# A new order table for every engine of a transformer layer, with the rests of the softmax weights shared out anew

## What is computed

```python
q, k = rope(x @ wq + bq), rope(x @ wk + bk)          # 16 heads of 8
scores = einsum('bhqd,bhkd->bhqk', q, k) / sqrt(8) + causal
attn = softmax(scores) @ (x @ wv + bv)
x = layernorm(x + attn @ wo + bo)
logits = x @ wg; idx = argmax(softmax(logits))         # top-1 of 8 experts
mask = one_hot(idx) * (locations < 512)                # place of the token in its expert
gate = sum(probs * mask)
x = layernorm(x + gate * (x @ W[idx].T + b[idx]))      # for the kept tokens
```

## Time and profile before

| | us |
|---|---|
| median of 3 runs (553.79 to 554.85) | 554.53 |
| the profiled execution | 555.73 |
| its span, first to last instruction | 554.0 |
| TensorE busy | 371.6 |
| VectorE busy | 362.1 |
| ScalarE busy | 246.1 |
| POOL busy | 299.2 |

### The profile page before, as it was taken

One profiled execution on the slowest core, in us unless ns is written; L12 is line 12 of the kernel. 1 busy time (PEld: TensorE's weight loads), 2 busy tenths in 40 slices (PEclk: granted clock), 3 DMA queues, 4 the chain that ended last, 5 costly groups with the idle time before them and its releaser, 6 DMA issues.

```text
span 554.0 us, 13276 instructions
## 1 busy us (share of the span) xinstructions
PE 371.6 (67%) x4150; PEld 317.0 (57%) x4150; DVE 362.1 (65%) x929; ACT 246.1 (44%) x568; POOL 299.2 (54%) x524
## 2 busy tenths in 40 slices
PE   4456478676767768666775775776686576868572
PEld 3344367565746657565655665664575565656551
DVE  5578466774857767584866758486675848584635
ACT  3434545444535345353534545344454445454510
POOL 6344646446383755638284654728465473636433
PEclk9586887988888788888898888889878888878687
DMA  4779548393938365483926547392837439501000
GB/s 115 127 148 128 115 115 98 92 114 98 116 74 136 61 123 63 100 105 92 128 54 127 60 121 78 97 123 64 140 51 133 55 98 115 99 2 43 11 9 21
DMA packets 155055, 50.53 MB, mean 91 GB/s; under 512 B 113567, under 2 KB 151331, under 8 KB 155022
## 3 DMA queue, kind: packets, MB, share of 16 engines
q1 hardware_dynamic: 149118, 45.80, 49.9%
q10 hardware_dynamic: 5184, 2.36, 2.2%
q0 software_dynamic: 720, 1.97, 1.2%
HBM read 30.70 MB, written 14.68 MB: 82 GB/s over the span
## 4 chain that ended last, share of the span: by engine, by line
POOL 28%; issue 21%; DVE 18%; PE 15%; SPq 7%; ACT 5%; DMA 3%; POOLq 1%; DVEq 1%; ACTq 0%
DVE low L868 4%; POOL rs L476 4%; DVE row_max L877 4%; POOL low L515 4%; SPq L419 3%; POOL rot L596 3%; POOL rot_rest L602 2%; POOL y_out L489 2%; POOL all_parts L504 2%; POOL two_parts L502 2%; PE ps_ab L1083 2%; PE ps_m L1019 2%; DVE z L843 2%; PE ps_n L1130 1%; PE ps_m L1020 1%
## 5 line engine op out<-in xcount | busy, mean ns | idle before, releaser
L674 ACT ACTIVATE high<-ps_ab 128x448 f16<-128x448 f32 (+1 forms) x192 | 101.2, 527 | 151.8 <-PE ps_ab L1083 146.9
L877 DVE TENSOR_REDUCE row_max<-ps_ab 128x2 f32<-128x512 f32 (+3 forms) x176 | 108.7, 635 | 73.3 <-PE ps_ab L1093 73.3
L515 POOL TENSOR_TENSOR low<-probs,high 128x448 f16<-128x448 f32 (+1 forms) x80 | 78.7, 984 | 39.2 <-ACT probs L681 39.1
L1063 PE MATMUL ps_ab<-mask_b_bf,ident_bf 128*128 128x128 bf16 (+1 forms) x192 | 51.9, 270 | 58.5 <-DVE low L868 58.3
L1109 PE MATMUL ps_pv<-v_mov,high 128*128 128x64 bf16 x768 | 76.4, 204 | 9.0 <-DVE low L868 8.6
L868 DVE TENSOR_TENSOR low<-ps_ab,high 128x448 f16<-128x448 f32 (+1 forms) x112 | 67.0, 598 | 20.4 <-ACT ps_ab L681 20.4
L1083 PE MATMUL ps_ab<-q_plain,k_diag 128*128 128x128 bf16 (+1 forms) x768 | 78.5, 234 | 0.0
L1109 PE MATMUL ps_pv<-v_mov,low 128*128 128x64 bf16 x768 | 75.3, 203 | 0.0
L1093 PE MATMUL ps_ab<-k_plain,q_diag 128*128 128x192 bf16 (+3 forms) x512 | 74.6, 265 | 0.0
L1109 PEld LDWEIGHTS ps_pv<-v_mov,high 128*128 128x128 f16 x768 | 63.0, 106 | 16.7 <-DVE low L868 10.4
L502 POOL TENSOR_TENSOR two_parts<-pv_rows 128x128 f32<-128x128 f32 x32 | 14.7, 459 | 105.6 <-DVE inv_den L853 105.3
(11 more groups left out here) (178 smaller groups left out, 939.4 us busy)
## 6 DMA issues: line engine op xcount, KB each, us to landing
plain_parts<-rot SPq DMA_DIRECT2D x180, 64.0 KB, 2.0
k_plain<-plain_parts SPq DMA_DIRECT2D x16, 384.0 KB, 3.8
q_diag<-plain_parts SPq DMA_DIRECT2D x32, 192.0 KB, 5.1
q_plain<-plain_parts SPq DMA_DIRECT2D x16, 384.0 KB, 6.0
k_diag<-plain_parts SPq DMA_DIRECT2D x32, 192.0 KB, 6.5
v_mov<-v_parts SPq DMA_DIRECT2D x64, 48.0 KB, 2.2
x_in<-in_L_attn_x_dram SPq DMA_DIRECT2D x16, 128.0 KB, 2.2
x_res<-in_L_attn_x_dram SPq DMA_DIRECT2D x16, 128.0 KB, 2.3
```

The source lines that it names most:

```text
L515: pool.tensor_tensor(fine(low, k), kept_probs(k), fine(high, k), ALU.subtract).then_inc(s_["low_pool"], 1)
L674: act.activation(fine(high, k), b_scores(k), ACT.Exp, scale=SCALE)
L877: last = dve.tensor_reduce(row_max[:, NBLK - 1 - j, groups[0]:groups[-1] + 1], scores[:, :, col:col + width(j)], AX.X, ALU.max)
L1063: return pe.matmul(v, ident_bf[:, :], rows, start=True, stop=False, skip_group_check=True)
```

## The change

Every program step is now divided into 64 slots, and a table for each engine (`PE_AT`, `ACT_AT`, `DVE_AT`, `POOL_AT`) gives each piece a position; `position // 64` is by how many program steps the piece lags behind the start of its sequence, and `position % 64` its slot. `due` finds what stands in a slot. `LAST_AT` holds other positions for the last two sequences. Only the order of each engine's list follows from the numbers. SyncE's list is as it was. Blocks 3 and 9 get their rests on another path: TensorE subtracts `high` from the bank by a product with minus the identity, and ScalarE copies the result out. Block 10's rest goes from POOL to VectorE and block 11's from VectorE to POOL. The routing mask moves from VectorE to ScalarE (`route`), the bias row of the projection becomes three bfloat16 rows, and `x1` gets two buffers. Core of the diff:

```diff
-LOW_POOL = (1, 3, 5, 8, 10)
-B_SLOT, LOW_SLOT, SLOTS = 1, 2, NB + 4
+LOWS = "DPDADPDDPADP"
+SLOTS = 64
+PE_AT = dict(
+    b=(201, 204, 207, 213, 220, 223, 228, 231, 236, 240, 241, 248),
...
+        def bank_free(eng, c, k):
+            if LOWS[k] == "P":
+                after(eng, "exp_done", c, NB, k + 1)
             else:
-                after(eng, "low_dve", c, N_DVE, dve_lows(k) + 1)
+                low_ready(eng, c, k)
...
+                    for k, c, _, _ in due(ACT_AT, "low", *now):
+                        if LOWS[k] == "A":
+                            after(act, "subtracted", c, lows_of("A"), lows_of("A", k + 1))
+                            act.activation(fine(low, k), b_scores(k), ACT.Copy).then_inc(s_["low_act"], 1)
...
+                    for _, d, _, _ in due(ACT_AT, "route", *now):
+                        after(act, "loc_ready", d, 1, 1)
+                        after(act, "kept_done", d, 1, 1)
+                        act.activation(route[0:E, :], ps_route, ACT.Copy, bias=-BIG, scale=BIG).then_inc(s_["route_done"], 1)
...
+                    for k, c, _, _ in due(PE_AT, "sub", *now):
+                        if LOWS[k] == "A":
+                            after(pe, "exp_done", c, NB, k + 1)
+                            pe.matmul(b_scores(k), minus_ident[:, :], fine(high, k), start=False, stop=True,
+                                      skip_group_check=True).then_inc(s_["subtracted"], 1)
...
-                            mm = pe.matmul(ps_n[:, 128 * t:128 * t + 128], row_0[:, :], out_row[:, :],
+                            mm = pe.matmul(ps_n[:, 128 * t:128 * t + 128], rows_1[:, :], out_rows[:, :],
```

More of the change, by code:

```diff
@@ L665, in step @@
             def step(s, p, half):
[L666 removed]
                 for slot in range(SLOTS):
[L668 to L671 removed]
+                    now = s, slot, p, half
+                    for k, c, _, _ in due(ACT_AT, "b", *now):
                         after(act, "b_ready", c, NB, k + 1)
@@ L704, in step @@
                                        ACT.Copy).then_inc(s_["v1_done"], 1)
-                    if slot == 11 and has(b):
+                    for _, b, pb_, _ in due(ACT_AT, "maxrows", *now):
                         after(act, "ex_ready", b, 1, 1)
@@ L1095, in step @@
                         mm.then_inc(s_["a_ready"], 1)
-                    if slot == 12 and has(d) and not (is_step(s, B) or is_step(s, B + 1)):
-                        experts(d, n, 0)
-                    for k in PV_IN.get(slot, ()) if has(c) else ():
+                    for k, c, q, _ in due(PE_AT, "pv", *now):
                         low_ready(pe, c, k)
@@ L1121, in step @@
                         mm.then_inc(s_["ex_ready"], 1)
-                    if slot == SLOTS - 1 and has(d) and not (is_step(s, B) or is_step(s, B + 1)):
-                        experts(d, n, 1)
-                    if slot == SLOTS - 1 and is_step(s, B):
-                        experts(d, n, 0)
-                    if slot == 2 and has(d):
+                    for k, d, _, _ in due(PE_AT, "e", *now):
+                        if not is_step(d, B - 1):
+                            experts(d, k // 2, k % 2)
+                    for _, d, _, _ in due(PE_AT, "turn", *now):
                         after(pe, "normed", d, 2, 2)
-                        after(pe, "maxrows_done", b)
+                        after(pe, "maxrows_done", d + 2)
                         for t in range(2):
@@ L1131, in step @@
                         mm.then_inc(s_["turned"], 1)
-                    if slot == 4 and has(d):
+                    for _, d, _, _ in due(PE_AT, "y", *now):
                         after(pe, "attn_done", d, 1, 1)
@@ L1193, in step @@
                                 expert_terms(d, 0, h)
-                    if slot == 10 and has(d):
+                    for _, d, _, _ in due(PE_AT, "loc", *now):
                         after(pe, "chosen_done", d, 1, 1)
```

548 lines of the change are left out of this document (286 added, 262 removed).

## The result

The changed kernel takes 446.89 us (median of 4 runs, 443.04 to 448.38), the kernel before 554.69 us beside it: a ratio of 0.8046, 95% interval 0.7993 to 0.8099. The forecast was 459.

What follows compares the result with a forecast made beforehand. The prediction took a ring of waits between engines, not any engine's load, to bound the kernel: 50.3 us ahead, 15 steps of 24.4 (366.0), 42.5 behind, together 458.8, so 459 us; range 430 to 512.

Steps and rivals of the forecast that it cites:

- The sum: Whole kernel: 50.3 us to the first block 0 exponential, 15 steps of 24.4, then 42.5 behind the last; together 458.8.
- Start and end: Time ahead of the first sequence's block 0 exponential, put at 50.3 us, and behind the last's, put at 42.5.
- The ring: Loop waits from one second `normalise` to the next through `output`, `rs1`, `x1`, logits and experts set the step: 24.4 us.
- bare ring: Rival, 14%: TensorE at 2.4 GHz throughout and hand-overs hidden, so a loop step of 22.7 us; 431 us in all.
- the additions: Added to each loop step: 1.0 us for TensorE's partly lower clock, 0.8 for a dozen hand-overs of some 0.07.
- The stretch from block 9's exponentials to the third experts' piece: Part of a loop step, charged to TensorE's list: subtraction, experts pieces, block 11, maxima and weighted sums; 3.91 us.
- The loads: Busy time per loop step after the change: VectorE about 20.5 us, POOL about 17.3, ScalarE some 16, TensorE 22.4.
- The subtraction: TensorE's new product for the rests of blocks 3 and 9, put at 0.25 us each, between 0.23 and 0.39.
- By themselves they move nothing: Claim that loads falling by about 1 us on two engines give no gain, since no load bounds the step.
- The clock: Rival, 5%: TensorE's clock stays down in the loop, granted 0.55, step 33.4 us, 594 us; slower than before below 0.61.
- Transfers bind: Rival, 14%: a DMA share of no more than 0.65 can be had, so a loop step of 27.9 and 511 us.
- The rule on shared interfaces: GpSimd and VectorE share SBUF interfaces; POOL losing time beside VectorE's rests: 0.12 us a step, 461 us, left out.

Runs made afterwards that it cites:

- output_first: The changed kernel with one move on POOL: `output` stands ahead of the second half of `normalise` again; 478.74 us, ratio 0.8635.
- old_rests: The changed kernel with the rests shared out between POOL and VectorE as before the change, none by subtraction and copy; 485.0 us, ratio 0.8772.
- before_normalise_first: The kernel before with one move on POOL: the second half of `normalise` stands ahead of `output`; 557.92 us, ratio 1.0067.
- no_scalar_rests: The changed kernel with the rests of blocks 3 and 9 on VectorE, no subtraction on TensorE, no copy on ScalarE; 440.53 us, ratio 0.7937.
- after_again: The changed kernel, unedited, measured once more to compare with later runs on the same chip; 442.67 us, ratio 0.7982.

## Why the prediction was right

The sum was 50.3 + 15 x 24.4 + 42.5; measured were 51.0 + 15 x 23.30 + 44.3. Start and end were 0.7 and 1.8 us too short, the step 1.1 us too long, 16.6 in all. The order gave the gain as forecast; that the number came within 3% also rests on parts that were off and cancelled.

- **The ring.** The prediction said that it is wrong in the ring if the loop's chain does not pass through `normalise`, `output`, `rs1` and the experts; the chain does. POOL's terms came out as read from the kernel before: `output` 4.11 (4.11), `rs1` 222.27 to 223.32, 1.05 (1.05), the rest 0.93 (0.91). The bare ring was put at 22.7 and is 22.81. That the place of `output` carries 32 us of the gain is shown by output_first, that the places of the rests matter, by 38 us, by old_rests, and that the one move is worth nothing by itself by before_normalise_first. Whether the two add up, and how the rest of the 108 us divides among the other moves, was not tested.
- **The terms that were mis-sized: the additions.** Together 1.0 us for the clock and 0.8 for hand-overs were charged to every step (the sum with them is 24.5; the 24.4 is a slip of rounding, 1.5 us in the end). Measured, the terms with their hand-overs make up the 22.81. No row was given for the 0.07 us of a hand-over; from POOL's last instruction of `normalise` to TensorE's turn it is 0.06 (217.19 to 217.25). Nor is the clock spread: in the changed kernel a step has it in full (1.00, 22.8 us) or loses 1.5 us at one place (0.93, 24.4 us). The x1 transpose and the logits had moreover been read at the lower level in the kernel before, 0.36 us for a logits product where it is 0.26 to 0.28 now. TensorE's stage table, in half microseconds of the long step (stretch, us, TensorE busy with its instructions, clock; the last two columns are of the transfers and are not read here):

```profile
248.50:249.00 0.50, 0.00 (x0) 1.00 0.00 0
249.00:249.50 0.50, 0.25 (x3) 1.00 1.44 197
249.50:250.00 0.50, 0.50 (x9) 0.66 0.53 180
250.00:250.50 0.50, 0.50 (x9) 0.50 0.89 360
252.50:253.00 0.50, 0.50 (x4) 0.50 1.73 126
253.00:253.50 0.50, 0.50 (x15) 0.93 1.94 117
```

  The clock falls to the lower level behind the pause ahead of the logits (0.99 us, the longest that is left in a step), and the q and k products that follow run at half speed until 253. So the forecast of 24.4 has the length of the long step, by chance, since it came by another way, and the "bare ring" rival of 22.7 that of the short one; the 446.89 us lie between the two, since both occur.
- **Terms that cancelled.** `x1` was charged 1.30 and takes 0.60, since no POOL rest runs beside it now; from the transpose of `x1` to the logits it is 226.43 - 224.01 = 2.42 instead of 1.71; the logits' four products take 0.47 for 0.86 at the upper clock. The stretch from block 9's exponentials to the third experts' piece was charged 3.91 to TensorE's list, and is 235.09 - 231.12 = 3.97 (231.12 is the end of the last exponential), but the chain passes there through VectorE (`add` 1.74). From that piece to the next `normalise` it is 238.44 - 235.09 = 3.35 for 2.98. That these differences, up to 0.7 us, add up to 0.1 is luck.
- **The loads.** VectorE and POOL were put at 20.5 and 17.3 and have 21.0 to 21.5 and 17.4, ScalarE 16.0 for "some 16". The subtraction was put at 0.25 and takes 0.34 to 0.36 (two of 32 take 0.55), still nothing on TensorE's total. "By themselves they move nothing" holds for the two rests on ScalarE (no_scalar_rests), but not in general: a rest that lands at a bad place takes others with it (old_rests, 38 us).
- **Rivals.** The clock was 0.923 over the span, not at 0.6. "Transfers bind" was looked for in the wrong number: the DMA engines' share went to 0.79 and 0.80, past the 0.74 forecast and the 0.65 of the rival, but SyncE's list of 24 issues, 22.8 us with 1.4 of waiting for its own writes, is as long as the ring. (The copies of the row maxima do not stand in SyncE's queue, as the rival had it: the page has a second queue, q10, with 2.36 MB, which by size are ScalarE's transfers; the 16 engines are shared.) The list could have been read in the trace of before: a step of 32.2 less 11.0 of waiting. That would have given some 21 us, not 22.8: the first issue of `v_mov` takes 3.17 us now, right behind the others, where it took 0.67 after the wait of 11 us. So a part of the list is not the bare price of issuing: something holds that issue, and whether full DMA engines do was not tested. With a shorter ring all this would have been the error of the forecast.
- **The rule on shared interfaces.** The trace agrees with the Trainium skill, "GPSIMD Engine Reference", section "1. Specifications", but the prediction applied it to the wrong instructions. The rests on VectorE, with one operand in PSUM, hardly stretch; `add` and `gate_kept`, with two tensors in SBUF, do. So does `x1`, with one tensor; the section also names a two-port mode, and no run here shows whether `x1` uses it. Two rows of the changed kernel (one line's instructions: minimum, median and maximum in ns):

```profile
L908 DVE TENSOR_TENSOR low<-ps_ab,high x96: 546/615/626, 52.0 to 416.9; 128x448 f16<-128x448 f32 x64, 128x384 f16<-128x384 f32 x32
L883 DVE SCALAR_TENSOR_TENSOR z<-y_sel,gate_kept,xn x30: 340/353/1475, 107.3 to 431.4; 128x128 f32<-128x128 f32 x30
```

  The rows also show how it comes about: such an instruction is not slowed in proportion, it ends when POOL's running one ends. `gate_kept`, two columns wide, ends at 225.24 with POOL's rest at 225.22, and takes 0.15 where POOL is idle; `add` ends at 233.12, behind POOL's rotation at 232.97. In the kernel before this held up `x1` on the ring (1.30 for 0.60 now). In the changed kernel it holds up `add` (1.74 for 0.61) and `gate_kept` (0.84, as before, but it now stands on the chain ahead of the logits): together some 1.8 us of holding a step for 0.7 before, not 0.12 us more. A part of the 2.42 us above is this.

What stays open: why SyncE's first issue of `v_mov` takes some 3 us of the 5.17 (the four took 2.83 in the kernel before), what decides in which steps the clock falls, and how much the row maxima's way by transfer binds: in the second profile of the changed kernel (after_again) it is on the chain in the loop too.

## What to carry to other kernels

Where no engine is full, sum up one ring from a wait back to itself, with every engine's list in its new order; such a sum came within 0.1 us of the short step here, with parts off by up to 0.7 that cancelled. Then do the same for the queue that issues the transfers: time spent issuing is no wait and no busy time in the table of engines, and a list that waited 11 us a step was the next bound here. When two edits that each shorten one ring show little, try them together before they are dropped.

## What the runs showed of the hardware

- Some VectorE instructions with operands in SBUF only are held until POOL's running instruction on SBUF ends: in the changed kernel `add` takes 0.34 us alone and up to 1.48 beside POOL's rotation, `gate_kept` 0.15 and up to 0.87; `x1` takes 0.34 alone, and 1.05 beside a rest in the kernel before (per instruction). Rests that read PSUM kept their time (0.55 to 0.63).
- A pause of 0.99 us on TensorE was followed by 3.4 us at the lower clock, once 6.8, in some steps and by none in others with the same pause.
- Issuing is not free: twelve transfers of 64 KB took SyncE 8.8 to 9.0 us, two on ScalarE 1.6, and the output's transfer held POOL for 0.81 with 0.71 of waiting ahead of it.
